# Fused layer kernel: the q/k/v projection in fp16 parts with its loop written out, and attention with three score and three back banks

## What is computed

```python
# L0 attention: masked product of two weights, gelu, added to x and normalised
attn = einsum('ds,td->st', w1, w2) * sparse_mask
y = gelu(einsum('bds,st->bdt', x, attn) + b2)
# L0 ffn: quantised weights plus a low-rank term
w = (q - 7.5) * (scale * 0.005); lin = x @ w.T + 0.02 * (x @ A @ B)
h = silu(gate(x)) * up(x); y = down(h)
# L1 attention: 32 heads of 16, 8 key/value heads, rotary, causal; of chunks of 16 keys
# only the best 8, the first 128 and the last 128 keys are allowed
q, k, v = x @ wq.T, x @ wk.T, x @ wv.T
q, k = q * cos + rotate_half(q) * sin, k * cos + rotate_half(k) * sin
p = softmax(where(allowed, q @ k.T / 4, NEG)); y = (p @ v) @ wo.T
# L1 ffn: eight LoRA branches, routed by a softmax
```

## Time and profile before

| | |
|---|---|
| three executions | 1399.55, 1403.16, 1405.0 us; median 1403.16 |
| profiled execution | 1402.04 us, span 1400.1 us, 30498 instructions |
| PE busy | 1238.9 us (88%) |
| DVE busy | 977.2 us (70%) |
| ACT busy | 802.8 us (57%) |
| POOL busy | 352.4 us (25%) |
| setup, gated, project | to about 105, 475 and 593 us |
| attention, output | to about 1272 us, and the end |

### The profile page before, as it was taken

How to read it: one execution, slowest core, us unless ns; L and a number is a source line. 1 busy time by engine, 2 the same in 40 slices (tenths; PEclk the granted TensorE clock), 3 DMA queues, 4 the chain that set the end, 5 groups by cost and what they waited for, 6 DMA issues and landing times. The chain is left out here.

```text
span 1400.1 us, 30498 instructions
## 1 busy us (share of the span) xinstructions
PE 1238.9 (88%) x10462; PEld 686.4 (49%) x10558; DVE 977.2 (70%) x3122; ACT 802.8 (57%) x1477; POOL 352.4 (25%) x884
## 2 busy tenths in 40 slices
PE   8958999999999699569999999999999999995995
PEld 3423444434444355345555555555555555553663
DVE  5885655746564344468888888888888988872784
ACT  2623643526243156447777777777777767773564
POOL 3431000000000233322222222222222222233575
PEclk9985999999999899869999999999999999998998
DMA  9401000000000034450111110111111011001231
GB/s 328 186 1 45 1 1 0 0 0 0 0 0 1 6 56 84 86 94 6 24 27 28 27 28 5 28 24 28 27 28 27 6 23 28 14 9 46 61 91 54
DMA packets 144967, 53.50 MB, mean 38 GB/s; under 512 B 133516, under 2 KB 135692, under 8 KB 144192
## 3 DMA queue, kind: packets, MB, share of 16 engines
q1 hardware_dynamic: 144832, 51.74, 16.3%
HBM read 29.19 MB, written 12.06 MB: 29 GB/s over the span
## 5 line engine op out<-in xcount | busy, mean ns | idle before, releaser
L1302 ACT ACTIVATE arena<-bank 128x512 f32<-128x512 f32 x576 | 329.1, 607 | 162.6 <-PE bank L1222 76.0
L1363 DVE TENSOR_REDUCE arena<-bank 128x32 f32<-128x512 f32 x528 | 339.2, 679 | 63.9 <-PE bank L1209 51.4
L1209 PE MATMUL bank<-arena 96*128 96x512 f16 (+3 forms) x832 | 225.5, 320 | 6.0 <-DVE arena L1370 2.1
L1222 PE MATMUL bank<-arena 113*128 113x512 f16 x576 | 219.0, 385 | 11.4 <-ACT arena L1302 5.8
L1242 PE MATMUL bank<-arena 128*32 128x128 f32 x4608 | 165.6, 277 | 16.0 <-ACT arena L1302 15.7
L1455 POOL TENSOR_SCALAR arena<-arena 128x128 bf16<-128x128 bf16 x384 | 142.6, 371 | 141.0 <-DVE arena L1418 119.9
L585 PE MATMUL bank<-arena 128*128 128x512 f16 (+1 forms) x704 | 171.4, 387 | 0.0
L1242 PEld LDWEIGHTS bank<-arena 128*32 128x32 f32 x4608 | 114.1, 109 | 50.9 <-ACT arena L1302 28.3
L597 PE MATMUL bank<-arena 128*128 128x512 f16 (+1 forms) x528 | 118.5, 387 | 3.1 <-ACT arena L657 3.1
L1449 POOL TENSOR_TENSOR arena<-arena 128x4 f16<-128x4 f32 x128 | 27.2, 213 | 349.8 <-DVEq L1398 332.2
L585 PEld LDWEIGHTS bank<-arena 128*128 128x128 f16 (+1 forms) x704 | 71.5, 102 | 85.5 <-issue 6.9
(11 more groups left out here) (183 smaller groups left out, 2012.1 us busy)
## 6 DMA issues: line engine op xcount, KB each, us to landing
arena<-arena SPq DMA_DIRECT2D x32, 256.0 KB, 2.9
arena<-qk_rows SPq DMA_DIRECT2D x16, 480.0 KB, 5.9
qk_rows<-arena SPq DMA_DIRECT2D x16, 384.0 KB, 3.6
arena<-in_x SPq DMA_DIRECT2D x4, 1024.0 KB, 13.1
out<-arena SPq DMA_DIRECT2D x16, 256.0 KB, 2.1
arena<-in_down_qT SPq DMA_DIRECT2D x1, 2816.0 KB, 25.3
arena<-in_up_qT SPq DMA_DIRECT2D x1, 2752.0 KB, 19.1
arena<-in_gate_qT SPq DMA_DIRECT2D x1, 2752.0 KB, 30.8
```

The source lines that it names most:

```text
L1209: last = pe.matmul(bank[:, at:at + k1 - k0], query_aug[st.slot][0:WIDE, h * P:(h + 1) * P], key_aug[st.p][0:WIDE, k0:k1], start=True, stop ...
L1222: last = pe.matmul(bank[:, :], key_aug[st.p][0:KROWS, j * P:(j + 1) * P], query_aug[st.slot][0:KROWS, :], start=True, stop=not extra)
L1302: act.activation(probs[u % PROBS], back_bank[u % 2][:, :], ACT.Exp, scale=float(HD) ** -0.5).then_inc(probs_ready, 1)
L1363: dve.tensor_reduce(out=cm[:, number * per:(number + 1) * per], in_=score_bank[bank_of_score(front, number)][:, :].rearrange("p (c d) -> p ...
```

## The change

In `gated` POOL scales the projection's weights by 64 and cuts them into a high and a low fp16 part, after `rstd_all` and ahead of its groups. In `project` x is kept in fp16 (`x_high`, four buffers), DVE makes its rest from the bank (`x_rest`), and each product is the sum of three fp16 ones, twelve matmuls of each width a tile. The loops are written out, and the tiles go in order 0 to 15, so batch 0 is done after four rounds. PE's order in a round becomes turns of pair i+1, then products of pair i; ACT's becomes keep i+1, normalise i+2, evacuate i, cut i; DVE's begins with the rests of pair i+1. The staged buffers get a place of their own; their gaps are blanked in `project`, and the rows of groups 0 and 1 are loaded in its fifth round. The wait for the last rows moves to the load of group 8 in `attention`, which gets three score and three back banks. The output weights' parts and three buffers of the last stage move.

```diff
                     branch_rstd(pool, m, pool_seq, t % 2).then_inc(branch_rstd_ready, 1)
+            w, w_high, w_rest = qkv_weights(m)
+            pool.wait_ge(m.qkv_in, 16)
+            pool_seq.mark(pool.tensor_scalar(out=w, in0=w, scalar1=W_UNIT, scalar2=None, op0=ALU.mult))
+            pool_seq.wait(pool)
+            pool_seq.mark(pool.tensor_copy(w_high, w))
+            pool_seq.wait(pool)
+            pool_seq.mark(pool.tensor_tensor(out=w_rest, in0=w, in1=w_high, op=ALU.subtract))
+            pool_seq.wait(pool)
+            pool_seq.settle()
             over_groups(pool, group)
...
+def load_rows(sp, m, dram, g):
+
+    p = g % 2
+    sp.dma_start(m.staged[p].rearrange("p (v r) -> p v r", r=WIDE)[:, :, 0:ROWS],
+                 dram["rows"][g].rearrange("p (v r) -> p v r", r=ROWS)).then_inc(m.staged_in[p], 16)
...
-    W = m.f32(WQKV_AT, DC * QKV)
-    take = m.taker(WORK, ARENA - SEQ)
-    xn, xT = [take(D) for _ in range(2)], [take(D) for _ in range(2)]
+    _, w_high, w_rest = qkv_weights(m)
+    take, rows_take = m.taker(WORK, ROWS_AT), m.taker(ROWS_AT, STAGED_AT)
...
+    x_high, x_rest = ([take(D, F16) for _ in range(4)] for _ in range(2))
...
-            with sp.Fori(0, SEQ_TILES) as i:
+            for i in range(SEQ_TILES):
                 for b in range(2):
                     k = i * 2 + b
-                    to = dram["rows"][b * KV:(b + 1) * KV].rearrange("k p (t w) -> p k t w", t=SEQ_TILES)[:, :, ds(i, 1), :].squeeze(2)
+                    batch, tile = divmod(k, SEQ_TILES)
+                    to = dram["rows"][batch * KV:(batch + 1) * KV].rearrange("k p (t w) -> p k t w", t=SEQ_TILES)[:, :, tile, :]
                     sp.wait_ge(high_rows_ready, k + 1)
                     sp.wait_ge(rows_ready, k + 1)
                     sp.dma_start(to[:, :, 0:GQ * ROWS], q_rows[b].rearrange("p (k w) -> p k w", k=KV)).then_inc(rows_out[b], 16)
                     sp.dma_start(to[:, :, GQ * ROWS:], k_rows[b].rearrange("p (k w) -> p k w", k=KV)).then_inc(rows_out[b], 16)
-            for b in range(2):
-                sp.wait_ge(rows_out[b], SEQ_TILES * 32 + 32)
+                if i == SEQ_TILES // 2:
+                    for b in range(2):
+                        sp.wait_ge(rows_out[b], SEQ_TILES // 2 * 32 + 32)
+                    for g in range(2):
+                        load_rows(sp, m, dram, g)
...
             def turn(k, b):
                 pe.wait_ge(xn_ready, k + 1)
+                if k >= 2:
+                    pe.wait_ge(x_rest_ready, k - 1)
                 for dc in range(DC):
                     last = pe.transpose(m.banks[b][:, dc * P:(dc + 1) * P], xn[b][:, dc * P:(dc + 1) * P], m.ident)
                 last.then_inc(turned, 1)
...
             def feed(k, b):
-                pe.wait_ge(xT_ready, k + 1)
+                pe.wait_ge(x_high_ready, k + 1)
                 pe.wait_ge(v_ready, k + 1)
-                for dc in range(DC):
-                    pe.matmul(m.banks[2 + b][:, :], xT[b][:, dc * P:(dc + 1) * P], W[:, dc * QKV:dc * QKV + D],
-                              start=dc == 0, stop=dc == DC - 1)
-                for dc in range(DC):
-                    last = pe.matmul(m.banks[4 + b][:, 0:QKV - D], xT[b][:, dc * P:(dc + 1) * P], W[:, dc * QKV + D:(dc + 1) * QKV],
-                                     start=dc == 0, stop=dc == DC - 1)
+                terms = [(x, w, dc) for x, w in ((x_high[k % 4], w_high), (x_high[k % 4], w_rest), (x_rest[k % 4], w_high)) for dc in range(DC)]
+                for bank, first, end in ((m.banks[2 + b], 0, D), (m.banks[4 + b], D, QKV)):
+                    for n, (x, w, dc) in enumerate(terms):
+                        if n == 2 * DC and first == 0:
+                            pe.wait_ge(x_rest_ready, k + 1)
+                        last = pe.matmul(bank[:, 0:end - first], x[:, dc * P:(dc + 1) * P], w[:, dc * QKV + first:dc * QKV + end],
+                                         start=n == 0, stop=n == len(terms) - 1)
                 last.then_inc(products, 1)
 
-            pe.wait_ge(m.qkv_in, 16)
             for b in range(2):
                 turn(b, b)
-            with pe.Fori(0, SEQ_TILES - 1) as i:
+            for i in range(SEQ_TILES - 1):
+                for b in range(2):
+                    turn(i * 2 + (2 + b), b)
                 for b in range(2):
                     feed(i * 2 + b, b)
-                for b in range(2):
-                    turn(i * 2 + (2 + b), b)
             for b in range(2):
...
         def _(act):
             def normed(i, b):
-                act.activation(xn[b], m.x(i + b * SEQ_TILES), ACT.Identity, bias=m.shift[:, ds(i + b * SEQ_TILES, 1)],
-                               scale=m.rstd[:, ds(i + b * SEQ_TILES, 1)]).then_inc(xn_ready, 1)
+                k = i * 2 + b
+                act.activation(xn[b], m.x(k), ACT.Identity, bias=m.shift[:, k:k + 1], scale=m.rstd[:, k:k + 1]).then_inc(xn_ready, 1)
 
             def keep(k, b):
                 act.wait_ge(turned, k + 1)
-                act.activation(xT[b], m.banks[b][:, :], ACT.Copy).then_inc(xT_ready, 1)
+                act.activation(x_high[k % 4], m.banks[b][:, :], ACT.Copy).then_inc(x_high_ready, 1)
 
             def evacuate(i, b):
                 k = i * 2 + b
                 act.wait_ge(products, k + 1)
                 act.wait_ge(rotated_ready, k + 1)
-                act.activation(raw[b][:, 0:D], m.banks[2 + b][:, :], ACT.Copy)
-                act.activation(raw[b][:, D:QK], m.banks[4 + b][:, 0:QK - D], ACT.Copy).then_inc(raw_ready, 1)
-                v = v_all.rearrange("p (b k t c) -> p b k t c", b=BATCH, k=KV, t=SEQ_TILES)[:, b]
-                act.activation(v[:, :, ds(i, 1), 0:HD].squeeze(2), heads(m.banks[4 + b][:, QK - D:QKV - D]), ACT.Copy).then_inc(v_ready, 1)
+                act.activation(raw[b][:, 0:D], m.banks[2 + b][:, :], ACT.Copy, scale=1.0 / W_UNIT)
+                act.activation(raw[b][:, D:QK], m.banks[4 + b][:, 0:QK - D], ACT.Copy, scale=1.0 / W_UNIT).then_inc(raw_ready, 1)
+                v = v_all.rearrange("p (b k t c) -> p b k t c", b=BATCH, k=KV, t=SEQ_TILES)[:, k // SEQ_TILES]
+                act.activation(v[:, :, k % SEQ_TILES, 0:HD], heads(m.banks[4 + b][:, QK - D:QKV - D]), ACT.Copy,
+                               scale=1.0 / W_UNIT).then_inc(v_ready, 1)
...
@@ -907,13 +946,16 @@
                 normed(0, b)
             for b in range(2):
                 keep(b, b)
-            with act.Fori(0, SEQ_TILES - 1) as i:
+            for b in range(2):
+                normed(1, b)
+            for i in range(SEQ_TILES - 1):
                 for b in range(2):
-                    normed(i + 1, b)
+                    keep(i * 2 + (2 + b), b)
+                if i + 2 < SEQ_TILES:
+                    for b in range(2):
+                        normed(i + 2, b)
                 for b in range(2):
                     evacuate(i, b)
-                for b in range(2):
-                    keep(i * 2 + (2 + b), b)
                 for b in range(2):
                     cut(i, b)
             for b in range(2):
...
-            pool_seq.settle()
-            with pool.Fori(0, SEQ_TILES) as i:
+            pool.memset(m.staged[1].rearrange("p (v r) -> p v r", r=WIDE)[:, :, ROWS:WIDE], 0.0)
+            for i in range(SEQ_TILES):
...
+            def keep_rest(k, b):
+                dve.wait_ge(x_high_ready, k + 1)
+                dve.tensor_tensor(out=x_rest[k % 4], in0=m.banks[b][:, :], in1=x_high[k % 4], op=ALU.subtract).then_inc(x_rest_ready, 1)
+
...
+            for b in range(2):
+                keep_rest(b, b)
             dve.wait_ge(rows_in, 16)
             for k in range(2):
                 dve.memset(m.key_aug[k][32:MASK_AT, :], 0.0)
                 dve.tensor_copy(m.key_aug[k][MASK_AT:KROWS, :], key_rows[MASK_AT:KROWS, :])
-            with dve.Fori(0, SEQ_TILES) as i:
-                dve_seq.enter(i, 4)
-                cos = m.cos.rearrange("p (t d) -> p t d", d=HD)[:, ds(i, 1), :]
+            dve.memset(m.staged[0].rearrange("p (v r) -> p v r", r=WIDE)[:, :, ROWS:WIDE], 0.0)
+            for i in range(SEQ_TILES):
+                if i < SEQ_TILES - 1:
+                    for b in range(2):
+                        keep_rest(i * 2 + (2 + b), b)
                 for b in range(2):
-                    k = i * 2 + b
-                    dve.wait_ge(raw_ready, k + 1)
-                    dve_seq.mark(dve.tensor_tensor(out=heads(rotated[b]), in0=heads(raw[b]),
-                                                   in1=cos.to_broadcast([P, QK // HD, HD]), op=ALU.mult))
-                    dve_seq.wait(dve)
-                    dve.wait_ge(spun_ready, k + 1)
-                    dve.tensor_tensor(out=rotated[b], in0=rotated[b], in1=spun[b], op=ALU.add).then_inc(rotated_ready, 1)
+                    rotate(i, b)
                 for b in range(2):
...
+                    cut_low(i, b)
...
```

(27 more changed lines are left out.)

62 lines of the change are left out of this document (40 added, 22 removed).

## The result

The changed kernel takes **1387.52 us**, median of four runs (1386.22 to 1388.76), beside 1403.92 for the kernel before: ratio 0.9899, 95% interval 0.9879 to 0.9918. The profiled execution took 1386.22 us with a span of 1384.4; the span before was 1400.1.

What follows compares the result with a forecast made beforehand. TensorE was taken to bound the projection; in attention no engine was full. From the profiled 1402.0 us, -9 - 3 - 5.7 + 11.5 - 10.5 = -16.7 gave 1385.3, with half the difference to the median 1386 us; range 1370 to 1401.

Steps and rivals of the forecast that it cites:

- Weight parts, +11.5: Start of gated stage: GpSimd's three long operations hold up VectorE's two-input cuts, last sum at 136.3 instead of 124.83; +11.5 us.
- Rival 2: Gated stage: GpSimd's weight parts hinder nothing, total 1374 us; chance 0.13.
- Projection, -9: Projection: pair period falls from 12.10 to 11.4 us, set by ScalarE's loop through the rotation; -9 us (-3 to -15).
- rival 3: Projection: the period falls to TensorE's 8.8 us a pair, 16 us less, total 1370 us; chance 0.06.
- Seam -3: Between projection and attention: SP's wait for the last row DMAs moves to the loading of group 8; -3 us.
- entry -5.7: Attention's start: groups 0 and 1 are loaded in projection's fifth round, so TensorE can begin at once; -5.7 us.
- With nothing of SP queued that another engine needs soon: Projection's fifth round: claimed the early loads of groups 0 and 1 delay no SP work another engine needs soon.
- Attention, -10.5: Attention: third masked-score bank saves 0.7 us a group against waits for exponentials; three score banks lose 0.1; -10.5 us.
- Output stage, 0: Output stage after attention: no change predicted, 0 us.
- Rivals 4: Projection: waiting TensorE loses 2.4 GHz, a pair takes 17.6 us, +37, total 1423; chance 0.11 together with rival 5.
- rival 5: Attention: with three score banks VectorE runs dry once per pair of steps, +41, total 1438; chance 0.11 with rival 4.
- a fall of the clock in the projection: Projection: sign named as showing the forecast wrong, if the clock falls there; no size given with the sign.

Runs made afterwards that it cites:

- experiment 3: Changed kernel with GpSimd's work on the projection's weights cut into twelve pieces and moved into the gated stage's last group: 1376.28 us, ratio 0.9827 to the kernel before.
- experiment 5: Changed kernel with ScalarE evacuating the first tile before keeping and normalising, and VectorE's remainders between first product and add: 1379.45 us, ratio 0.9855.
- experiment 9: Changed kernel with the projection's products in fp32 as before; written-out order, early loads and banks kept: 1382.02 us, ratio 0.9866 to the kernel before.
- experiment 10: Changed kernel with the two first row loads back at the head of attention, behind a wait for all rows: 1395.53 us, ratio 0.9971.
- experiment 4: Changed kernel with only the first group's rows loaded in round five, the second group's load back in attention: 1384.45 us, ratio 0.9889.
- experiment 7: Changed kernel with weight parts in pieces, one load in round five, ScalarE's new projection order and output buffers moved, all together: 1363.83 us, ratio 0.9737.
- experiment 1: Changed kernel with attention's banks as before, four for scores and two for masked scores: 1398.13 us, ratio 0.9976 to the kernel before.
- experiment 11: Kernel before with only attention's banks changed, three for scores and three for masked scores, with matching counts: 1394.76 us, ratio 0.9951.
- experiment 2: Changed kernel with the output stage's six late buffers moved by 453 words: 1385.26 us, ratio 0.9893 to the kernel before.
- experiment 6: Changed kernel with 22 more GpSimd adds, second operand at different offsets: adds took 1088 to 1092 or 1262 to 1263 ns; kernel time not compared.

## Why the prediction was right, step by step

The total, 1386 against 1387.5, was right and so was the sign of every term. That it came so close is in part luck: the gated stage cost 1.7 us less than I had put and the projection gave 1.0 more, while the attention gave 1.4 less and a cost of 2.9 was missing. And the attention's term is a difference of two sizes that were both far too small.

- **Weight parts, +11.5; measured +9.8,** and +9.5 by the last sum. Place, engine and mechanism as forecast, and experiment 3 gives 9.4 back when they stand elsewhere in pieces. One cut stands behind each of the three operations; the cuts were late to 118.7, 123.2 and 129.6, and I had put 120.5, 124.0 and 130.8. Half a microsecond of each is the stage's earlier start. The rest of the difference has two causes. I had let GpSimd's next operation wait for the held cut; by its records it begins 0.06 and 0.09 us after the one before. And the first cut ended 1.2 us before the record of GpSimd's scaling does (behind cast and subtraction it ends 0.55 us after them), so that one cut more, at 119.38, got through: held were cuts 2, 4 and 5, not 2, 3 and 4, and four sums were left behind them, not five. They follow each other at 1.39 us; by the 1.2 that I had written, my own last sum would have stood near 135.6, not at 136.3. Rival 2 fell. The rule of the Trainium skill ("SBUF — State Buffer", Who interferes with whom) held here: cut held, sum from a bank not.
- **Projection, -9; measured -10.1** at VectorE's end. Period 11.4 forecast, 11.1 measured; the rotation of both tiles 6.5 forecast (4 x 0.82 + 4 x 0.85 is 6.7), 6.1 measured (537.21 to 543.31). That ScalarE's loop through it is the bound is shown by experiment 5: other order, same work, 9.11 us. TensorE's 8.8 us a pair was right too (9.1 when full), so rival 3 described a kernel one edit away. What I did not say is that little of the period's gain was the fp16 parts' (experiment 9): of the 1.01 us that a pair lost, writing the loop out in the new order brings 0.79.
- **Seam -3 and entry -5.7; measured -2.9 and -5.9**, and 8.7 to 9.7 come back in experiment 10.
- **"With nothing of SP queued that another engine needs soon": wrong.** The two loads take SyncE's queue 7.27 us; I had reckoned with their landing only. ScalarE waited 1.6 us for the rows' transfers behind them, which cost 0.8 (experiment 4), and 5.3 us once the projection was faster, which cost 3.8 (experiments 5 and 7).
- **Attention, -10.5; measured -9.1**, 7.3 with the banks alone and a slower start. The mechanism holds (experiments 1, 11), its two sizes do not. I counted 0.7 us a group from the waits for exponentials and 0.1 lost on score banks. These waits fell by (48.1 - 11.8) / 16 = 2.3 us a group and the waits for reductions rose by (28.6 - 3.2) / 16 = 1.6. The difference, 0.7, is my number, but by luck; a middle group is only 0.5 shorter, and the last one gave 2.3. The nearest pair of score and reduction in one stretch said too little about a ring of three banks.
- **Output stage, 0; measured +2.9.** I had taken the new addresses of xn, xT and zn as no edit. They made GpSimd's add 178 ns longer a tile, 16 x 0.178 = 2.8 us (experiments 2 and 6).
- **Rivals 4 and 5.** The clock fell in one pair only, and that cost nothing, for TensorE was not its bound. I had named a fall of the clock in the projection as a sign that the forecast is wrong; that sign was too strict. VectorE did not run dry: its reductions' idle time is 54.3 us on the page after, 63.9 before.

## What to carry to other kernels

Before an engine is made faster, ask which queue the loop closes through: here cheaper products brought 0.2 us a pair, reordering the queue of ScalarE, which waited in the middle of its own list, 2.0 more. Work on an idle engine is free only if it doesn't hold up a busy one; cut in pieces and placed where the busy one has slack, the same work left the stage at 369.7 us, beside 369.3 before. A move of a buffer is an edit: compare the mean time of every line between two traces, the untouched ones too.
